# A fused gated cross-attention and expert layer: the first attention's keys made by a weight product, another order on every engine, zeros from another queue

## The chip, the core and the metric

The kernel runs on one core of one Trainium2 chip. The metric is the device time of one execution in microseconds (us), the median of several. A core has four engines that compute: TensorE (PE, matrix products; its weight loads are shown as PEld), VectorE (DVE), ScalarE (ACT) and GpSimd (POOL). A fifth, SyncE (SP), only issues transfers here. Each engine takes its own instructions in the order in which they are written, and waits on semaphores for the others.

## The reference

Eight sequences (B) of 256 tokens of width 256 pass four residual blocks. Each block normalises x first and is scaled by the tanh of a gain.

```python
x = x + tanh(g_xattn[0]) * L0_xattn(layernorm(x), ctx)   # one head, keys from ctx, 120 rows
x = x + tanh(g_ffn[0])   * L0_ffn(layernorm(x))          # 8 experts and 4 identities, best 2
x = x + tanh(g_xattn[1]) * L1_xattn(layernorm(x), ctx)   # 16 heads
x = x + tanh(g_ffn[1])   * L1_ffn(layernorm(x))          # rounded to 8 bits
# L0_xattn:
q = query @ Wq + bq;  k = key @ Wk + bk;  v = value @ Wv + bv
out = softmax(q @ k.T) @ v
```

The change is about the first line and what runs beside it. The scores are (xn Wq + bq)(ctx Wk + bk)^T. A term that is the same for all keys of a query drops out in the softmax.

## The kernel before, in words

Tokens lie on 128 partitions, two tiles (U) for a batch. Everything runs out of one program with a written order for each engine; a number t counts the iterations of a software pipeline, and each engine handles, in iteration t, steps of different batches.

**First attention.** For each batch b, TensorE makes keys `kt0` = Wk^T ctx (`keys0`, line 1549), which ScalarE copies out with the bias (`copy_kt0`, 622). Then TensorE multiplies them with Wq (`keys_by_query`, 1560) and with bq (1563), and VectorE copies the two results (`copy_kq`, 1006, `copy_bqk`, 1010). TensorE makes the values (1570), transposes the normalised x (1575, copied out by ScalarE in 629), and forms the scores (the bias row 1589, the product 1595). VectorE takes the maximum (1021), ScalarE the exponentials (635), TensorE transposes them (1604), ScalarE copies (642), TensorE multiplies with the values (1612), VectorE adds the result to x (1027, 1030).

**Norms.** VectorE makes mean and variance (986 to 994; `stats0` of x, `stats1` of x after the attention), GpSimd takes the root (496, 498; `root0`, `root1`), ScalarE applies it (648 for `norm0`, 657 for `norm1`). The second result is stored to HBM by SP, transposed (1575 again, copied by VectorE in 1041) and multiplied with the gate (1629); VectorE adds the gate's bias (1051) and has the logits.

**Choice of experts.** From the logits VectorE finds the two best experts of each token (`highest`, `mark_highest`, `keep_first`, `leave`; 1071 to 1083), for the first twelve tiles already inside the loop, for the last four and for the second choice after it. It forms `pairs` (1135), counts them with TensorE's help and turns them into slots (1175) and block numbers (1182). GpSimd then gathers the tokens of each of 39 blocks, TensorE runs the experts, and the second attention and the last layer follow.

**Beside it.** The expert weights (8 MB) come in eight loads of 1 MB from SP's queue. They are used as a sum of two parts, so they are split in 32 pieces of 512 columns: ScalarE writes the high part (`high`, 667), after the load, and GpSimd the low part (`low`, 512), after the high part; VectorE takes four of the low ones (1047). Which iteration takes how many pieces is written by hand (`HIGH_FROM`, `LOW_FROM`, `LOW_LATE`). The rows to which the experts' results are added start as zeros: ScalarE's queue writes them (`clear_y`), four transfers of 1 MB, in iteration 7. TensorE waits for all low parts behind the slot products, then issues a few products as a warm-up (1706), and reads the block numbers.

In iteration t the order before was as in the functions below. On ScalarE the first pieces stand in iteration 2, behind the normalisation of batches 0 and 1.

Of the kernel before, what the change touches and what calls it, by code (L numbers as in the profile page):

```python
# [90 lines left out]
def build(nc, x, ctxT, wq0T, wk0, wv0, bq0, bk0, bv0, gateT, gbias, wmoe, wq1, wk1, wv1, wo1,  # L91
          bq1, bk1, bv1, bo1, wfT, bf, gains, c_ident, c_tri, c_count, c_token, c_head, out):
    ctx = ExitStack()
    with ctx:
# [87 lines left out]
        kt0 = sb("kt0", [P, 2, C, LK], F32, att)  # L182
# [111 lines left out]
        def sems(names):  # L294
# [11 lines left out]
        (kt_done, kt_ok, kq_done, kq_ok, bqk_ok, v0_done, v0_ok) = sems(  # L306
            "kt_done kt_ok kq_done kq_ok bqk_ok v0_done v0_ok")
# [7 lines left out]
        split_h, split_l, split_d = sems("split_h split_l split_d")  # L315
# [80 lines left out]
        IN_CTX, IN_CON, IN_CST = 16 * 3, 16 * 4, 16 * 6  # L396
# [9 lines left out]


        HIGH_FROM, LOW_FROM = (8, 2, 2, 2), (4, 4, 9, 3)
        EARLY, FAR = TILES - 2 * U, 64 * P
        AHEAD, ZERO_LOADS = 6, 1 + 2 * TILES * D // ZEROS  # L410
        VECTOR_LOW, VECTOR_FROM = (7, 10, 13, 16), 5
        LOW_LATE = {B: 3, B + 1: 4, B + 2: 3, B + 3: 2, B + 4: CHUNKS}

        @block.sync
        def _(sp):
# [58 lines left out]
        def _(pool):  # L474
            pool.dma_start(ident[:], c_ident).then_inc(cst_in, 16)
# [38 lines left out]
            pieces = iter(j for j in range(CHUNKS) if j not in VECTOR_LOW)  # L514

            def low_next(t, k):

                if t >= LOW_FROM[k]:
                    for j in itertools.islice(pieces, 1):
                        low(j)  # L520

            for t in range(B):
                low_next(t, 0)
                low_next(t, 1)
                root0(t)
                low_next(t, 2)
                low_next(t, 3)
                if 0 <= t - 5:
                    root1(t - 5)
            for t in range(B, B + 5):  # L530
                root1(t - 5)
                for j in itertools.islice(pieces, LOW_LATE[t]):
                    low(j)
# [73 lines left out]
        def _(act):  # L607
# [10 lines left out]
            def copy_kt0(b):  # L618
                act.wait_ge(kt_done, b + 1)
                wait(act, kq_done, b - 1)  # L620
                for m in range(C):
                    ins = nc.scalar.activation(kt0[:, b % 2, m, :], bank[5][:, m * LK:(m + 1) * LK], ACT.Identity,
                                               bias=bk0_sb[:, m:m + 1])
                ins.then_inc(kt_ok, 1)
# [46 lines left out]
            def high_next(t, k):  # L671

                if t >= HIGH_FROM[k]:
                    for j in itertools.islice(pieces, 1):
                        high(j)

            def clear_y():

                act.wait_ge(zero_ok, 1)
                act.dma_start(xn_d[0:1, :], wh[0:1, E_FFN * WE - D:].bitcast(F32)).then_inc(zeroed, 16)  # L680
                y_p = y_d[1:1 + 2 * TILES * P, :].rearrange("(p r) n -> p (r n)", p=P)
                for c in range(0, 2 * TILES * D, ZEROS):
                    act.dma_start(y_p[:, c:c + ZEROS], wh[:, E_FFN * WE - ZEROS:].bitcast(F32)).then_inc(zeroed, 16)

            for t in range(B + 9):
                if t == B - 1:
                    clear_y()
                if t < B:
                    copy_kt0(t)
                high_next(t, 0)  # L690
                high_next(t, 1)
# [7 lines left out]
                if 0 <= t - 3 < B:  # L699
                    copy_probT(t - 3)  # L700
                high_next(t, 3)
                if 0 <= t - 1 < B:
                    copy_xT(t - 1)
# [276 lines left out]
        def _(dve):  # L980
# [22 lines left out]
            def copy_kq(b):  # L1003

                dve.wait_ge(kq_done, b + 1)
                dve.tensor_copy(kq[:, cols(b, C * LK)], bank[1][:, 0:C * LK]).then_inc(kq_ok, 1)

            def copy_bqk(b):
                dve.wait_ge(kq_done, b + 1)
                dve.tensor_copy(bqk[0:1, cols(b, LK)], bank[1][0:1, C * LK:(C + 1) * LK]).then_inc(bqk_ok, 1)  # L1010

            def copy_v0(b):

                dve.wait_ge(v0_done, b + 1)
                dve.scalar_tensor_tensor(v0[:, b, 0:D], bank[4][0:LK, 0:D], gain[0:LK, 0:1], bv0g[0:LK, :], ALU.mult,
# [26 lines left out]

            def low(j):

                dve.wait_ge(split_h, j + 1)
                c = cols(j, CHUNK)
                dve.tensor_tensor(wl[:, c], wl[:, c].bitcast(F32), wh[:, c], ALU.subtract).then_inc(split_d, 1)
# [37 lines left out]
            for t in range(B + 9):  # L1085
                if t < B:
                    stats0(t)
                if 0 <= t - 3 < B:
                    copy_bqk(t - 3)
# [1037 lines left out]
```

## Time and profile before

| | us |
|---|---|
| median of 3 runs | 392.32 (391.3 to 392.92) |
| the profiled execution: its own time | 393.37 |
| its span, first to last instruction | 391.6 |
| last logits added | 77.8 |
| block numbers ready | 91.5 |

Busy shares of the span: PE 89%, PEld 69%, DVE 68%, ACT 59%, POOL 41%. Shares of the chain that ended last: PE 71%, DVE 9%, ACT 8%, DMA 5%, waiting for issue 4%. The weight loads move 413 to 439 GB/s while they run.

A row of the chain names what the end of the program hung on at that moment. A row in order of time gives start, length, engine, line, tile written and tiles read, and in brackets how long the engine had stood idle before and what released it. "x4" means four instructions merged in one row. An fp32 product is two passes of TensorE, and two instructions in the trace. Granted clock is a share of 2.4 GHz.

### The profile page before, as it was taken

To read this page: it belongs to the slowest core of one execution; us is meant where nothing else is said; L and a number is where in the kernel's file an instruction comes from. 1 tells how busy PE (TensorE), PEld (TensorE's weight loads), DVE (VectorE), ACT (ScalarE), POOL (GpSimd) and SP (SyncE) were. 2 spreads that over 40 slices of the span, in tenths; PEclk is the share of its full clock that TensorE was granted. 3 is DMA by queue.
4 is the path that set the end of the run, shared out by engine and by line. 5 is a ranking of instruction groups with operands and counts; after the bars stand their busy time and mean duration, and the time that the engine had idled before them with its cause. 6 is when DMAs were issued, how large, how long until landed. Compare 5 with 4: busy or idle time off the path is not lost.

```text
span 391.6 us, 9083 instructions
## 1 busy us (share of the span) xinstructions
PE 347.3 (89%) x2955; PEld 268.6 (69%) x2956; DVE 266.0 (68%) x677; ACT 230.8 (59%) x462; POOL 159.2 (41%) x215
## 2 busy tenths in 40 slices
PE   1979999966899999999999998879999999989174
PEld 1768878644688888888888884556666666756142
DVE  1637887894645665555454456878889988685896
ACT  2387799530455555555555542466778678747685
POOL 6386589703255555555556524421132033001000
PEclk9969999975899999999999999999999999999776
DMA  7998381311132343423322304310011000000014
GB/s 191 329 419 332 145 365 57 110 28 40 40 95 94 108 133 103 123 68 80 80 73 67 87 30 145 112 56 22 35 56 55 2 2 2 3 2 2 0 42 175
DMA packets 15387, 38.26 MB, mean 98 GB/s; under 512 B 3574, under 2 KB 4748, under 8 KB 13820
## 3 DMA queue, kind: packets, MB, share of 16 engines
q1 hardware_dynamic: 9978, 22.55, 16.2%
q0 software_dynamic: 3936, 10.45, 9.2%
q10 hardware_dynamic: 1442, 4.85, 3.2%
q8 instruction: 19, 0.31, 0.4%
q14 instruction: 12, 0.10, 0.1%
HBM read 24.34 MB, written 13.50 MB: 97 GB/s over the span
## 4 chain that ended last, share of the span: by engine, by line
PE 71%; DVE 9%; ACT 8%; DMA 5%; issue 4%; ACTq 1%; SPq 1%; POOL 0%; DVEq 0%
PE two L1738 14%; PE two L1872 5%; PE two L1726 5%; PE two L1727 5%; PE two L1728 5%; PE two L1757 4%; PE two L1937 4%; PE two L1902 4%; PE two L1858 3%; PE two L1838 3%; DMA wl<-in_wmoe 3%; PE two L1748 2%; PE two L1929 2%; PE two L1595 1%; ACT wh L667 1%
## 5 line engine op out<-in xcount | busy, mean ns | idle before, releaser
L539 POOL DMA_INDIRECT xg<-xn_d,slot_i x39 | 37.8, 968 | 65.3 <-PE two L1748 51.1
L1222 DVE SCALAR_TENSOR_TENSOR gate<-th,two 128x512 f32<-128x512 f32 x39 | 26.8, 687 | 42.8 <-ACT th L738 42.8
L1726 PE MATMUL two<-wh,gh 128*128 x156 | 47.3, 303 | 0.2
L545 POOL DMA_INDIRECT y_d<-y_sb,goal_i x39 | 38.5, 988 | 20.5 <-ACT y_sb L748 10.5
L738 ACT ACTIVATE th<-two 128x512 f32<-128x512 f32 x39 | 23.3, 597 | 35.5 <-PE two L1738 35.5
L1727 PE MATMUL two<-wl,gh 128*128 x156 | 44.0, 282 | 0.0
L1728 PE MATMUL two<-wh,gl 128*128 x156 | 43.9, 282 | 0.0
L1757 PE MATMUL two<-ident,gate 128*128 128x128 f32 x156 | 41.9, 272 | 0.0
L559 POOL TENSOR_TENSOR rstd<-var,half 128x2 f32<-128x2 f32 x14 | 9.8, 701 | 76.7 <-DVE var L1289 76.7
L1322 DVE TENSOR_REDUCE nm<-two 128x8 f32<-128x960 f32 x32 | 36.1, 1151 | 4.5 <-PE two L1858 4.1
L512 POOL TENSOR_TENSOR wl<-wl,wh 128x512 fp32r<-128x512 f32 x28 | 35.2, 1275 | 9.8 <-ACT wh L667 9.8
L1738 PE MATMUL two<-wl,xh 128*128 x78 | 38.0, 487 | 0.0
L1738 PE MATMUL two<-wh,xl 128*128 x78 | 37.9, 485 | 0.0
L1738 PE MATMUL two<-wh,xh 128*128 x78 | 35.0, 449 | 2.1 <-DVE xl L1216 2.1
L836 ACT ACTIVATE pT<-two 120x1024 f32<-120x1024 f32 x32 | 31.1, 1036 | 7.0 <-PE two L1872 7.0
L1216 DVE TENSOR_TENSOR xl<-two,xh 128x256 fp32r<-128x256 f32 x39 | 16.6, 425 | 23.2 <-ACT xh L733 23.1
L1726 PEld LDWEIGHTS two<-wh,gh 128*128 128x128 f32 x156 | 29.5, 189 | 3.3 <-issue 0.7
L1727 PEld LDWEIGHTS two<-wl,gh 128*128 128x128 f32 x156 | 29.7, 190 | 0.0
L1728 PEld LDWEIGHTS two<-wh,gl 128*128 128x128 f32 x156 | 29.6, 190 | 0.0
L733 ACT ACTIVATE xh<-two 128x256 fp32r<-128x256 f32 x39 | 15.0, 384 | 23.2 <-PE two L1748 23.1
L1226 DVE TENSOR_TENSOR gl<-two,gh 128x512 fp32r<-128x512 f32 x39 | 26.6, 683 | 0.8 <-ACT gh L743 0.8
L748 ACT ACTIVATE y_sb<-two 128x256 f32<-128x256 f32 x39 | 15.0, 384 | 19.7 <-PE two L1728 19.0
(267 smaller groups left out, 892.0 us busy)
## 6 DMA issues: line engine op xcount, KB each, us to landing
wl<-in_wmoe SPq DMA_DIRECT2D x8, 1024.0 KB, 14.5
y_d<-wh ACTq DMA_DIRECT2D x4, 1024.0 KB
yg<-y_d SPq DMA_DIRECT2D x7, 512.0 KB, 3.6
xn_d<-xq SPq DMA_DIRECT2D x8, 256.0 KB, 2.0
xz<-xn_d SPq DMA_DIRECT2D x8, 256.0 KB, 2.6
out_x<-of SPq DMA_DIRECT2D x8, 256.0 KB, 2.0
x_sb<-in_x SPq DMA_DIRECT2D x1, 1024.0 KB, 7.9
x_sb<-in_x SPq DMA_DIRECT2D x1, 768.0 KB, 4.5
```

Of the source, the lines that this page charges most:

```text
L512: pool.tensor_tensor(wl[:, c], wl[:, c].bitcast(F32), wh[:, c], ALU.subtract).then_inc(split_l, 1)
L539: pool.indirect_dma_start(xg[:, n % 2, :], None, xn_d, bass.IndirectOffsetOnAxis(ap=slot_i[:, n:n + 1], axis=0)).then_inc(gathered[n % 2], 16)
L545: pool.indirect_dma_start(y_d, bass.IndirectOffsetOnAxis(ap=goal_i[:, n:n + 1], axis=0), y_sb[:, n % 2, :], None).then_inc(y_stored[n % 2] ...
L836: nc.scalar.activation(pT[:, r, p, :], ring(ring_of_keys(b, r) + p)[0:LK, :], ACT.Exp).then_inc(e_ok, 1)
L1222: dve.scalar_tensor_tensor(gate[:, k, :], th[:], 1.0, bank[2 + k][:], ALU.add, ALU.mult).then_inc(gate_ok, 1)
L1226: dve.tensor_tensor(gl[:, k, :], bank[4 + k][:], gh[:, k, :], ALU.subtract).then_inc(gl_ok, 1)
L1322: dve.tensor_reduce(nm[:, u, 2 * HG * p:2 * HG * (p + 1)].rearrange("p (j h) -> p j h", j=2), src.rearrange("p j (h k) -> p j h k", k=LK), ...
L1726: pe.matmul(dst, gh[:, k, a], wh[:, bass.ds(w, D)], start=c == 0, stop=False)
L1727: pe.matmul(dst, gh[:, k, a], wl[:, bass.ds(w, D)], start=False, stop=False)
L1728: ins = pe.matmul(dst, gl[:, k, a], wh[:, bass.ds(w, D)], start=False, stop=c == FC - 1)
L1738: ins = pe.matmul(bank[2 + k][:], (xl if part == 2 else xh)[:, k, c * P:(c + 1) * P], (wl if part == 1 else wh)[:, bass.ds(e + c * FF, FF) ...
L1757: ins = pe.transpose(bank[4 + k][:, c * P:(c + 1) * P], gate[:, k, c * P:(c + 1) * P], ident[:])
```

## The change

It does five things.

- **Keys.** At the start TensorE transposes Wk, forms Wk Wq^T (`qk`, with Wk bq as its last column) and the small bias terms, and then makes the keys of all batches in two products of 480 columns for each half of the width, and the bias row in two more (`fold_keys`, `keys0`). VectorE copies half of it out and ScalarE the other half (`copy_fold`, `copy_kq0`, `copy_kq1`). The work for each batch in `keys0`, `keys_by_query`, `copy_kt0`, `copy_kq` and `copy_bqk` goes away. The identity gets a semaphore of its own.
- **Order.** The loops of TensorE, ScalarE and VectorE are written anew. Steps follow one another at fewer iterations of distance (B + 7 in place of B + 9), and VectorE makes the first statistics four batches ahead.
- **High pieces** of ScalarE: the counts for each iteration are the list `HIGHS`; the first piece now stands in iteration 0 ahead of `norm0(0)`.
- **Low pieces** all go to GpSimd. It takes the roots of batches 0 to 4 first, two pieces ahead of each of the roots 5 to 7, the pieces of the list `LOWS` between the roots of the second norm, and all that are left behind the last root.
- **Zeros.** SP's queue writes them, between the fifth and the sixth weight load.

In the diff, runs of removed lines are left out; they stand in the functions above.

```diff
+        HIGHS = (1, 1, 2, 2, 2, 2, 1, 1, 3, 3, 3, 3, 3, 3, 2)
+        LOWS = (2, 2, 1, 1, 1, 2, 2)
...
+                if m == LOADS // 2:
+                    sp.wait_ge(zero_ok, 1)
+                    sp.dma_start(xn_d[0:1, :], wh[0:1, E_FFN * WE - D:].bitcast(F32)).then_inc(zeroed, 16)
+                    y_p = y_d[1:1 + 2 * TILES * P, :].rearrange("(p r) n -> p (r n)", p=P)
+                    for c in range(0, 2 * TILES * D, ZEROS):
+                        sp.dma_start(y_p[:, c:c + ZEROS], wh[:, E_FFN * WE - ZEROS:].bitcast(F32)).then_inc(zeroed, 16)
...
+            pieces = iter(range(CHUNKS))
+            def low_next(n):
+                for j in itertools.islice(pieces, n):
                     low(j)
+            for b in range(5):
+                root0(b)
+            for b in range(5, B):
+                low_next(2)
+                root0(b)
+            for b in range(B):
+                if b:
+                    low_next(LOWS[b - 1])
+                root1(b)
+            for j in pieces:
+                low(j)
...
+            def copy_kq1():
+                act.wait_ge(fold_ok, 3)
+                for h in range(2):
+                    act.wait_ge(fold_done, 6 + h)
+                    nc.scalar.activation(keys_of_half(1, h), bank[4 + h][:, 0:HB].rearrange("p (b k) -> p b k", k=LK),
+                                         ACT.Identity, bias=kq_bias[:, 1:2]).then_inc(kq1_ok, 1)
...
+            def high_next(n):
+                for j in itertools.islice(pieces, n):
+                    high(j)
+            for t in range(B + 7):
                 if 0 <= t - 3 < B:
-                    exp0_of(t - 3)
+                    copy_probT(t - 3)
+                high_next(HIGHS[t])
                 if 0 <= t - 6 < B:
                     norm1(t - 6)
-                high_next(t, 2)
+                if 0 <= t - 1 < B:
+                    copy_xT(t - 1)
+                if t == 1:
+                    copy_kq1()
+                if 0 <= t - 2 < B:
+                    exp0_of(t - 2)
                 if t < B:
                     norm0(t)
...
+            def copy_fold():
+                dve.wait_ge(fold_done, 1)
+                dve.tensor_copy(wkT[:].rearrange("p c n -> p (c n)"), bank[5][:, 0:C * P]).then_inc(fold_ok, 1)
+                dve.wait_ge(fold_done, 2)
+                dve.tensor_copy(qk[:], bank[0][:, 0:D + 1]).then_inc(fold_ok, 1)
+                dve.wait_ge(fold_done, 3)
+                dve.tensor_copy(kq_bias[:, 0:C], bank[7][:, 0:C])
+                dve.tensor_copy(kq_bias[0:1, C:C + 1], bank[7][0:1, C:C + 1]).then_inc(fold_ok, 1)
+            def copy_kq0():
+                dve.wait_ge(fold_ok, 3)
+                for h in range(2):
+                    dve.wait_ge(fold_done, 4 + h)
+                    dve.tensor_scalar(keys_of_half(0, h), bank[2 + h][:, 0:HB].rearrange("p (b k) -> p b k", k=LK),
+                                      kq_bias[:, 0:1], None, ALU.add).then_inc(kq_ok, 1)
+                for h in range(2):
+                    dve.wait_ge(fold_done, 8 + h)
+                    dve.tensor_scalar(bqk[:, h * HB:(h + 1) * HB], bank[6 * h][0:1, 0:HB], kq_bias[0:1, C:C + 1], None,
+                                      ALU.add).then_inc(kq_ok, 1)
 
...
+            for t in range(-4, B + 7):
+                if t == 0:
+                    copy_kq0()
                     dve.wait_ge(wv_in, 32)
                     dve.wait_ge(gain_ok, 1)
                     own.mark(dve.tensor_tensor(bv0g[:], bv0_sb[:], gain[:, 0:1].to_broadcast([P, D]), ALU.mult))
@@ -1095,32 +1094,32 @@
                     dve.wait_ge(cst_in, IN_CST)
                     dve.tensor_tensor(before[:], over(count[:, 0:E_FFN], E_FFN), wide(count[:, 0:E_FFN], E_FFN),
                                       ALU.is_lt)
...
+                if 0 <= t < B:
+                    copy_v0(t)
+                if t == 7:
                     dve.wait_ge(gate_in, 32)
...
+                if 0 <= t - 7 < B:
+                    logits_of(t - 7)
+                if t == B + 4:
                     dve.wait_ge(logit_kept, EARLY // U)
                     highest(0, lg, 0, EARLY)
                     mark_highest(0, lg, 0, EARLY)
-                if t == B + 7:
+                if t == B + 5:
                     keep_first(0, 0, EARLY)
                     leave(0, EARLY)
                     highest(1, left, 0, EARLY)
                 if 0 <= t - 5 < B:
-                    stats1(t - 5)
+                    copy_xT1(t - 5)
                 if 0 <= t - 2 < B:
...
+                    stats1(t - 2)
+                if 0 <= t < B:
+                    max0_of(t)
+                if t + 4 < B:
+                    stats0(t + 4)
+                if t == -4:
+                    copy_fold()
+                if 0 <= t - 1 < B:
+                    add_x1(t - 1)
...
+            def fold_keys():
+                pe.wait_ge(ident_in, 16)
+                for c in range(C):
+                    ins = pe.transpose(bank[5][:, c * P:(c + 1) * P], wk0_sb[:, c * P:(c + 1) * P], ident[:])
+                ins.then_inc(fold_done, 1)
+                pe.wait_ge(wq_in, 32)
+                pe.wait_ge(fold_ok, 1)
+                for c in range(C):
+                    pe.matmul(bank[0][:, 0:D], wkT[:, c, :], wq0_sb[:, c, :], start=(c == 0), stop=(c == C - 1))
+                for c in range(C):
+                    ins = pe.matmul(bank[0][:, D:D + 1], wkT[:, c, :], bq0_sb[:, c:c + 1], start=(c == 0), stop=(c == C - 1))
+                ins.then_inc(fold_done, 1)
                 for m in range(C):
                     for c in range(C):
-                        pe.matmul(bank[1][:, m * LK:(m + 1) * LK], wq0_sb[:, c, m * P:(m + 1) * P], kt0[:, b % 2, c, :],
-                                  start=(c == 0), stop=(c == C - 1))
+                        pe.matmul(bank[7][:, m:m + 1], wq0_sb[:, c, m * P:(m + 1) * P], bk0_sb[:, c:c + 1], start=(c == 0),
+                                  stop=(c == C - 1))
                 for c in range(C):
...
+                    ins = pe.matmul(bank[7][0:1, C:C + 1], bq0_sb[:, c:c + 1], bk0_sb[:, c:c + 1], start=(c == 0),
+                                    stop=(c == C - 1))
+                ins.then_inc(fold_done, 1)
+            def keys0():
+                pe.wait_ge(fold_ok, 3)
+                for m in range(C):
+                    for h in range(2):
+                        pe.matmul(bank[2 + 2 * m + h][:, 0:HB], qk[:, m * P:(m + 1) * P], ctxT_sb[:, h * HB:(h + 1) * HB],
+                                  start=True, stop=True).then_inc(fold_done, 1)
+                for h in range(2):
+                    pe.matmul(bank[6 * h][0:1, 0:HB], qk[:, D:D + 1], ctxT_sb[:, h * HB:(h + 1) * HB], start=True,
+                              stop=True).then_inc(fold_done, 1)
...
+            fold_keys()
+            keys0()
+            for t in range(B + 7):
+                if t == B + 2:
+                    pe.wait_ge(con_in, IN_CON)
+                if 0 <= t - (B + 2) < 3:
+                    products1(t - (B + 2), t - (B + 1))
+                if 0 <= t - 6 < B:
+                    transpose_x1(t - 6)
+                if 0 <= t - 2 < B:
+                    transpose_prob(t - 2)
+                if 0 <= t - 1 < B:
+                    scores0(t - 1)
+                if t == 0:
+                    pe.wait_ge(set_up, 1)
+                if t < B:
+                    transpose_x0(t)
+                if 0 <= t - 2 < B:
+                    attend(t - 2)
+                if t == 0:
+                    pe.wait_ge(wv_in, 32)
+                if t < B:
+                    values0(t)
+                if t == 7:
                     pe.wait_ge(gate_in, 32)
...
                 if 0 <= t - 7 < B:
-                    transpose_x1(t - 7)
+                    gate_of(t - 7)
```

## Rows read from the trace of the kernel before

**Rows 1.** Chain of waits, 0 to 115 us: start us, us, what (x instructions)

```profile
9.50 9.94 DMA wl<-in_wmoe
...
31.36 0.44 PE two L1575 x4
31.80 0.89 PE two L1560 x8
32.69 0.50 PE two L1563 x4
33.19 0.36 PE two L1604 x2
...
33.99 0.44 PE two L1549 x4
34.43 0.60 PE two L1589 x2
35.02 1.08 PE two L1595 x8
...
36.98 0.44 PE two L1575 x4
...
54.75 0.81 PE two L1629 x8
...
70.04 0.81 PE two L1637 x2
```

**Rows 2.** Windows of 10 us: busy time of each engine, granted clock, DMA

```profile
20.00:30.00 10.00, 7.95 (x39) 6.32 (x38) 2.67 (x11) 8.12 (x20) 8.92 (x9) 0.66 1.01 422
```

**Rows 3.** Order in time on ScalarE, 58 to 64 us: start, us, instruction

```profile
58.62 0.59 ACT L629 ACTIVATE xT<-two 128x512 f32<-128x512 f32 x1
...
60.37 0.61 ACT L635 ACTIVATE prob<-two,negmax 128x120 f32<-128x120 f32 x2
60.88 1.08 ACT L657 ACTIVATE xq<-x_sb,less,rstd 128x256 f32<-128x256 f32 x2
...
62.38 0.37 ACT L642 ACTIVATE probT<-two 120x256 f32<-120x256 f32 x1
62.64 1.66 ACT L667 ACTIVATE wh<-wl 128x512 fp32r<-128x512 f32 x3
```

**Rows 4.** Order in time on VectorE, 52 to 58 us

```profile
53.92 0.69 DVE L1041 COPY xT<-two 128x512 f32<-128x512 f32 x1 [0.50 <-PE two L1575]
...
54.99 0.87 DVE L1030 SCALAR_TENSOR_TENSOR x_sb<-two,rsum,x_sb 128x256 f32<-128x256 f32 x2
...
55.90 0.75 DVE L986 BATCH_NORM_STATS2 stat<-x_sb 128x6 f32<-128x256 f32 x2
...
57.05 0.14 DVE L994 TENSOR_REDUCE var<-mean 128x2 f32<-128x4 f32 x1
```

**Rows 5.** Order in time on GpSimd, 70 to 75 us

```profile
71.70 0.69 POOL L496 TENSOR_TENSOR rstd<-var,half 128x2 f32<-128x2 f32 x1
72.47 0.20 POOL L498 TENSOR_TENSOR less<-less,rstd 128x2 f32<-128x2 f32 x1
72.62 1.27 POOL L512 TENSOR_TENSOR wl<-wl,wh 128x512 fp32r<-128x512 f32 x1
...
73.85 1.33 POOL L512 TENSOR_TENSOR wl<-wl,wh 128x512 fp32r<-128x512 f32 x1
```

**Rows 6.** Order in time on VectorE, 73 to 82 us

```profile
73.33 0.30 DVE L1071 TENSOR_REDUCE top<-logit 128x12 f32<-128x144 f32 x1
73.67 0.40 DVE L1074 TENSOR_TENSOR eq<-logit,top 128x144 f32<-128x144 f32 x1
...
74.09 1.26 DVE L1075 SCALAR_TENSOR_TENSOR cand<-eq,count 128x144 f32<-128x144 f32 x1
...
80.03 0.36 DVE L1075 SCALAR_TENSOR_TENSOR cand<-eq,count 128x192 f32<-128x192 f32 x1
...
81.20 0.29 DVE L1135 TENSOR_TENSOR pairs<-hot 128x128 bf16<-128x128 f32 x1
```

More of the change, by code:

```diff
@@ L512, in low @@
                 pool.tensor_tensor(wl[:, c], wl[:, c].bitcast(F32), wh[:, c], ALU.subtract).then_inc(split_l, 1)
[L514 to L532, printed above, removed]
-                    low(j)
+            pieces = iter(range(CHUNKS))
+            def low_next(n):
+                for j in itertools.islice(pieces, n):
+                    low(j)
+            for b in range(5):
[9 more added lines that the diff above has]
+                low(j)
             pool.wait_ge(slots_kept, 1)
@@ L616, in _ @@
             act.wait_ge(ctx_in, IN_CTX)
[L618 to L624, printed above, removed]
+            def copy_kq1():
[4 more added lines that the diff above has]
+                                         ACT.Identity, bias=kq_bias[:, 1:2]).then_inc(kq1_ok, 1)
             def copy_xT(b):
@@ L1083, in leave @@
                 then(dve.scalar_tensor_tensor(left[:, i:n], hot[:, 0, i:n], -3.0e38, lg[:, i:n], ALU.mult, ALU.add))
[L1085 to L1089, printed above, removed]
-                if t == 3:
+            for t in range(-4, B + 7):
+                if t == 0:
+                    copy_kq0()
                     dve.wait_ge(wv_in, 32)
@@ L1544, in _ @@
             pe.wait_ge(ctx_in, IN_CTX)
-            def keys0(b):
-                wait(pe, kt_ok, b)
-                for m in range(C):
-                    ins = pe.matmul(bank[5][:, m * LK:(m + 1) * LK], wk0_sb[:, m * P:(m + 1) * P], ctxT_sb[:, cols(b, LK)],
-                                    start=True, stop=True)
-                ins.then_inc(kt_done, 1)
-            def keys_by_query(b):
-                pe.wait_ge(kt_ok, b + 1)
-                wait(pe, kq_ok, b)
-                wait(pe, bqk_ok, b)
+            def fold_keys():
[10 more added lines that the diff above has]
+                ins.then_inc(fold_done, 1)
@@ L1558, in keys_by_query @@
                 for m in range(C):
                     for c in range(C):
-                        pe.matmul(bank[1][:, m * LK:(m + 1) * LK], wq0_sb[:, c, m * P:(m + 1) * P], kt0[:, b % 2, c, :],
-                                  start=(c == 0), stop=(c == C - 1))
+                        pe.matmul(bank[7][:, m:m + 1], wq0_sb[:, c, m * P:(m + 1) * P], bk0_sb[:, c:c + 1], start=(c == 0),
+                                  stop=(c == C - 1))
                 for c in range(C):
-                    ins = pe.matmul(bank[1][0:1, C * LK:(C + 1) * LK], bq0_sb[:, c:c + 1], kt0[:, b % 2, c, :],
-                                    start=(c == 0), stop=(c == C - 1))
@@ L1567, in values0 @@
             def values0(b):
                 wait(pe, v0_ok, b)
-                wait(pe, xT1_copied, b - 5)
-                pe.matmul(bank[4][0:LK, 0:D], ctxT_sb[:, cols(b, LK)], wv0_sb[:], start=True, stop=True).then_inc(v0_done, 1)
+                pe.matmul(bank[1][0:LK, 0:D], ctxT_sb[:, cols(b, LK)], wv0_sb[:], start=True, stop=True).then_inc(v0_done, 1)
             def transposes(dst, src):
```

112 lines of the change are left out of this document (15 added, 97 removed).

## The prediction, made before the changed kernel was run

> **What bounds the kernel now.** I read the page first (the table above), then the chain of waits, then the order in time on each engine between 20 and 92 us, because the diff touches nothing behind that. The first attention with its gate ends at 77.8 us, a chain of VectorE instructions turns the logits into a list of slots and blocks until 91.5, and then TensorE runs the experts almost without a gap. So the change is worth what it moves the moment at which block numbers are ready and the split weights are whole. Inside the attention the reader should see the chain stay on TensorE from 31 to 42 us: one batch takes 5.62 us (transposes start at 31.36 and again at 36.98) and the engine does not stop between them [rows 1]. Before that the chain hangs on a load: the first of the eight weight loads lands at 19.44 [rows 1], and behind this wait TensorE's clock drops to the 1.2 GHz level for a while: granted 0.66 between 20 and 30 us [rows 2]. After that stretch it is at 2.4 GHz.
>
> **Part 1, keys for all batches ahead.** Per batch TensorE loses the key product by query (0.89), its bias row (0.50) and the raw key product (0.44) [rows 1]: 1.83 of 5.62, so 3.79 remains, 14.6 for eight batches. What comes instead is done once: two transposes, the 128x257 product, twelve one-column matmul passes, and six products of 480 columns. One like these takes 0.81 (the row at 70.04, one product in two passes [rows 1]), so 4.9 at 2.4 GHz, at most twice that at 1.2; the small ones I put at 3 to 5, from the 0.50 of the four bias passes, doubled. Starting at about 6 (identity and first weights are in by then) they end between 14 and 21; I take 18.6. It costs nothing if it ends before 21.1, for this reason: in iteration 0 ScalarE now has a first piece of the weight split ahead of the normalisation of batch 0, and that piece waits for the load that lands at 19.44. Before, two batches were normalised by then. So batch 0 is transposed from 21.1, behind an idle TensorE, at the low clock. With the key copies of ScalarE (two of 480 columns, some 0.65 each) ahead of the scores I get scores(0) complete at 27.1; between the bounds 25.8 (high clock) and 28.
>
> **Part 2, the loop from there.** The order is now tighter. Between the end of one batch's scores and the next stand: transpose of the next x, ScalarE's copy of it (0.59), exponentials (0.61), transpose of the probabilities (about 0.36), bias row and scores (0.60 + 1.08) [rows 1, 3], with semaphores about 4.0. ScalarE itself has, per iteration, 0.37 + 0.59 + 0.61, a normalisation of 1.08 and from batch 6 on a second one, and the split pieces at 0.55 each in a row [rows 3]; that is 3.6 to 4.2. VectorE has in iterations 2 and 3 two sets of statistics (55.90 to 57.19, so 1.29 each), the residual (0.87 and a reciprocal) and some 0.9 of small work [rows 4]: 4.5. TensorE has 3.79, and 5.04 once the second transpose (0.44) and the gate (0.8) join. Taking the longest each time, and the waits between engines in the written order, the seven intervals are 4.5, 3.8, 4.2, 4.6, 4.8, 4.2 and 5.1: scores(7) complete at 58.3. Before it was at 63.9, so the attention gains 5.6 there. Then a part is given back: three split pieces stand in each of ScalarE's iterations 8 to 13. From the last exponentials (60.3) it has 0.9 (wait and copy) + 1.7 + 1.1, then three times 1.7 + 1.0: the last normalised x1 is out at 72.0. Transpose (0.65), copy (0.69 [rows 4]), gate (1.0) and add bring the last logits to 74.6, against 77.8: 3.2 earlier. ScalarE alone bounds it below: it has some 45.5 of work from 19.4 to that last normalisation, so no earlier than 65 plus 2.6. VectorE loses its four split pieces, but they lie beside TensorE's work. The zeros go from ScalarE's queue to SP's, between the fifth and sixth load. They are 4 MB, about 10 us at the 413 GB/s of the table, so the last loads land near 50 and the pieces in them are wanted from 61 on; this costs nothing, and ScalarE need not issue them. SP's stores of x1 start at about 46, behind these loads, and are wanted two batches later.
>
> **Part 3, GpSimd's order, where I see the price.** Before, it had done 25 of its 28 pieces when the last root was taken at 71.70. Now it has all 32. The root of batch 4 waits for statistics that VectorE makes behind the first maximum, near 28.9, so nothing is split before that. Up to the last root, 6 + 11 = 17 pieces are placed: all 15 others stand behind root 7. That root needs the last x1's statistics; in VectorE's order they stand behind the copy of batch 4's transpose, so the root starts at about 67.3 and ends at 68.2 to 68.4 (0.69 + 0.20 with gaps [rows 5]). 15 pieces of 1.27 to 1.33 [rows 5] run till 87.9 at least, all through the chain of VectorE that chooses the experts, which before had GpSimd silent from 76.5.
> Does that matter? The trace shows it at one place. GpSimd's pieces run from 72.62 to 73.89 and from 73.85 to 75.18 [rows 5]. VectorE's equality begins at 73.67 and ends at 74.07, 0.2 behind the end of the first; the next operation begins at 74.09 and ends at 75.35, again 0.2 behind the end of the second: 1.26 us for 144 columns, where the same line does 192 columns in 0.36 with GpSimd silent [rows 6]. The reduction ahead of them, and copies out of PSUM at other times, are not stretched. So an instruction of that kind is let in once per piece. GpSimd loses only 0.03 to 0.06 by it.
> The Trainium skill (SBUF — State Buffer, section "Who interferes with whom") says that a VectorE instruction with two SBUF inputs and a GpSimd instruction that reads SBUF exclude each other for a whole instruction, while a reduction is outside of this. The trace agrees in the two operations above (1.26 against 0.36). By the rows alone only the equality and the multiply-add are proven to be stopped, which would be 6 instructions of the stage; by the rule the products and differences too, 12 in all. With six the total below would be about +2 instead of +7.
> I take all that read two SBUF tiles, since the equality is the same instruction type as the others. Early part: equality and multiply-add (iteration 12) end at about 72.5 and 73.8; the copy of the last transpose stands behind them, 74.5; equality and difference of iteration 13 at 76.4 and 77.7; the last logits are added at 78.2 instead of 74.6. Of the 3.2 nothing is left (+0.4). Late part, from there: eight such instructions in a row of dependence (equality, multiply-add, mark, leave, difference, equality, multiply-add, mark), one per 1.30, with the reductions inside these gaps: 79.0, 80.3, 81.6, 82.9, 84.2, 85.5, 86.8, 88.1. By then GpSimd is done, and the pairs are formed at 88.2 instead of 81.20 [rows 6]. All behind it is as before.
> **Sum:** +7.0 on the profiled execution (393.4 us by its own time, span 391.6), which was 1.05 above the median. On the median of 392.3 that is 399.3, so 399. The end of GpSimd's pieces (87.9) isn't waited for then: slots would be ready at 96.9.
>
> **Rivals.**
> *A: the two engines hardly meet; faster.* For it: two stretched instructions are few, and the attention's gain may be larger. Then the blocks are ready 3.2 earlier, at 88.3. TensorE waits for all pieces ahead of its warm-up, at 87.9, and that just fits. Time: 392.3 - 3.2 = 389. It decides where fewer than about four of the twelve are stopped (they cost 10.2 together in my sum, 0.85 each). Against it: both meetings of that kind in this stretch end with GpSimd's piece.
> *B: the attention reaches ScalarE's bound,* last logits up to 7 earlier than in my walk, with the blocking in full: 399.3 - 7 = 392, no change. It would need ScalarE never to wait, where the first scores alone hold it for 3.
> *C: the clock.* TensorE now stands still between 18.6 and 21.1 and works in pieces until 29. If it stays at the low level for two iterations more, each has 7.6 instead of some 4.2: +6.8, so 406. For it: the 0.66 in the stretch behind the wait for the first load [rows 1, 2]. Against: with full work it was at the high level again by 29.
> *D: half of the instructions are stopped,* or GpSimd is a few pieces ahead: +1 to +3, so about 394.5.
>
> **Chances.** Forecast 0.58 (own range 395.5 to 403), A 0.17, B 0.07, C 0.10, D 0.08. Within 0.5% is 390.3 to 394.3, about what a measurement here can tell from no change: faster is A, same is B and part of D. The range goes from 389.5 to 405: it takes in most of A, and C with one and a half cold iterations.
>
> **What would show it.** Right: the last GpSimd piece ends near 88; the row of that multiply-add shows over 1 us at several places and the chain from the last logits to the pairs takes near 10 us instead of 3.4; the last normalised x1 at 72; first transpose of x at 21. Wrong: a chain of 3.4 again with GpSimd still busy (the mechanism falls), GpSimd done before 80 (the order in time falls), or granted clock under 0.9 after 30 us (C).

## The result, and the profile after

| | before | after |
|---|---|---|
| median, us | 392.44 (4 runs, 391.3 to 392.9) | 397.73 (4 runs, 396.5 to 401.7) |
| ratio, with its 95% interval | | 1.0158 [1.012, 1.0196] |
| span of the profiled execution | 391.6 | 399.9 |
| last logits added, start | 77.65 | 75.48 |
| pairs formed, start | 81.20 | 85.27 |
| last low piece of GpSimd ends | 76.5 | 86.4 |
| block numbers ready, start of the last instruction | 91.31 | 96.66 |

The change is slower by 5.3 us (397.73 against 392.44). 399 was forecast. Ratios, here and below, are formed from fast executions alone and are not the quotient of the two medians. The profiled execution after is the longest of its four, so its span shows 8.3 us more; the stage that the change touches accounts for 5.35 of them (block numbers), and this is what the medians differ by. The other 3 lie behind it (last part of this section).

First VectorE in order of time, in the changed kernel (start, us, engine, line, what). It answers to [rows 6].

```profile
70.74 0.41 DVE L1076 TENSOR_TENSOR eq<-logit,top 128x144 f32<-128x144 f32 x1
71.18 1.27 DVE L1077 SCALAR_TENSOR_TENSOR cand<-eq,count 128x144 f32<-128x144 f32 x1
...
73.51 0.31 DVE L1082 TENSOR_TENSOR hot<-cand,pick 128x144 f32<-128x144 f32 x1
73.85 1.26 DVE L1085 SCALAR_TENSOR_TENSOR left<-hot,logit 128x144 f32<-128x144 f32 x1
75.15 0.30 DVE L1073 TENSOR_REDUCE top<-left 128x12 f32<-128x144 f32 x1
75.48 0.18 DVE L1053 TENSOR_TENSOR logit<-two,gbias_sb 128x24 f32<-128x24 f32 x1
...
75.94 0.36 DVE L1076 TENSOR_TENSOR eq<-logit,top 128x48 f32<-128x48 f32 x1
76.34 1.19 DVE L1077 SCALAR_TENSOR_TENSOR cand<-eq,count 128x48 f32<-128x48 f32 x1
77.56 0.20 DVE L1081 TENSOR_REDUCE pick<-cand 128x4 f32<-128x48 f32 x1
77.80 0.96 DVE L1082 TENSOR_TENSOR hot<-cand,pick 128x48 f32<-128x48 f32 x1
78.79 1.19 DVE L1085 SCALAR_TENSOR_TENSOR left<-hot,logit 128x48 f32<-128x48 f32 x1
...
80.25 0.92 DVE L1131 TENSOR_TENSOR dif<-top 128x16 f32<-128x16 f32 x1
81.09 1.48 DVE L1076 TENSOR_TENSOR eq<-left,top 128x192 f32<-128x192 f32 x1
82.60 1.30 DVE L1077 SCALAR_TENSOR_TENSOR cand<-eq,count 128x192 f32<-128x192 f32 x1
...
84.33 0.91 DVE L1082 TENSOR_TENSOR hot<-cand,pick 128x192 f32<-128x192 f32 x1
85.27 1.23 DVE L1134 TENSOR_TENSOR pairs<-hot 128x128 bf16<-128x128 f32 x1
...
96.66 0.18 DVE L1181 SCALAR_TENSOR_TENSOR blk_i<-blk,blks 128x20 int32<-128x20 f32 x1
```

Then GpSimd in the same kernel, as [rows 5]: the last root, and the first and last of the pieces behind it.

```profile
66.33 0.69 POOL L508 TENSOR_TENSOR rstd<-var,half 128x2 f32<-128x2 f32 x1 [0.53 <-DVE var L989]
...
67.25 8.99 POOL L524 TENSOR_TENSOR wl<-wl,wh 128x512 fp32r<-128x512 f32 x7
...
82.32 4.04 POOL L524 TENSOR_TENSOR wl<-wl,wh 128x512 fp32r<-128x512 f32 x3
```

The reader should see that between 71 and 86.5 us the equality (1076), multiply-add (1077), mark (1082), leave (1085), difference (1131) and pairs (1134) take 0.9 to 1.5 us, where with GpSimd silent 0.2 to 0.4 is their length. GpSimd runs its 15 pieces through just this time, from 67.25 to 86.36. Of the twelve instructions that the prediction counted, nine are stopped in full. The equality at 70.74 (0.41) meets the end of a piece, the mark at 73.51 (0.31) is not held, and the equality at 75.94 takes 0.36, where 0.21 was its length before. The pairs at 85.27 are stopped too (1.23 for 0.29) and make a tenth. The reductions between them (1073, 1081) keep their 0.2 to 0.3. From the start of the last logits to that of the pairs it takes 9.8 us; before it took 3.55.

The chain of waits of the changed kernel, start of the loop and the scores of batches 0, 1, 2 and 7 (start, us, what), to be read against [rows 1]:

```profile
9.38 10.22 DMA wl<-in_wmoe
...
19.68 0.63 ACT wh L676
20.31 0.99 ACT xq L657 x2
...
21.44 0.64 PE two L1585 x4
...
22.60 1.22 ACT kq L632 x2
...
24.59 1.16 PE two L1605 x8
...
29.57 1.99 PE two L1605 x8
...
36.17 1.10 PE two L1605 x8
...
57.12 1.08 PE two L1605 x8
```

The first weight piece on ScalarE waits for the load, and the norm of batch 0, its transpose and the key copies follow it. Scores(7) are complete at 58.2. And the granted clock (columns: stretch, length, busy us and count of PE, PEld, DVE, ACT, POOL; granted clock, DMA share, GB/s), against [rows 2]:

```profile
20.00:24.00 4.00, 1.79 (x9) 0.76 (x7) 2.37 (x5) 3.71 (x8) 0.00 (x0) 1.00 1.01 420
24.00:28.00 4.00, 3.66 (x17) 2.62 (x18) 2.02 (x8) 3.18 (x8) 0.53 (x1) 0.68 1.00 416
28.00:32.00 4.00, 4.00 (x16) 3.07 (x16) 0.40 (x2) 2.02 (x5) 2.81 (x4) 0.50 1.01 422
32.00:36.00 4.00, 4.00 (x12) 2.76 (x11) 2.94 (x13) 2.63 (x7) 2.64 (x4) 0.54 1.01 428
```

TensorE works 1.8 us of the 4 from 20 to 24, and then runs at the 1.2 GHz level until about 35.7, without a pause from 28 on. Before, the low stretch was over at 29. The same happens once more: in the window from 100 to 110 us, where the experts begin, the clock is 0.63 after the change, and 0.97 was granted from 100 to 110 before. These are different moments of the work (the experts begin 5.3 later), but between block numbers and the end the span is 303.2 after and 300.3 before. In ten of the twelve kernels below that distance is 300.1 to 301.6 (in the other two 301.9 and 302.0), so these 3 us are not taken as the change's. No run shows what decides them.

### The profile page after: what moved, and what is told of

Its sections match the earlier page's. It is cut to its first block, busy times and chain, and to the rows that moved or that the text cites. A ratio compares the mean times of both kernels' runs of the same rounds, so it can differ in the third digit from the quotient of the medians.

```text
span 399.9 us, 8859 instructions
## 1 busy us (share of the span) xinstructions
PE 353.4 (88%) x2861; PEld 266.9 (67%) x2862; DVE 270.5 (68%) x665; ACT 227.8 (57%) x448; POOL 164.0 (41%) x219
## 4 chain that ended last, share of the span: by engine, by line
PE 70%; DVE 12%; ACT 7%; DMA 5%; issue 3%; POOL 1%; SPq 1%; ACTq 0%; DVEq 0%
PE two L1736 14%; PE two L1870 5%; PE two L1724 5%; PE two L1725 5%; PE two L1726 5%; PE two L1755 4%; PE two L1900 4%; PE two L1935 4%; PE two L1856 4%; PE two L1836 3%; DMA wl<-in_wmoe 3%; PE two L1746 2%; PE two L1605 2%; PE two L1927 2%; PE two L1585 1%
## 5 line engine op out<-in xcount | busy, mean ns | idle before, releaser
L524 POOL TENSOR_TENSOR wl<-wl,wh 128x512 fp32r<-128x512 f32 x32 | 40.5, 1292 | 0.0
```

Source lines behind the costliest of these rows:

```text
L524: pool.tensor_tensor(wl[:, c], wl[:, c].bitcast(F32), wh[:, c], ALU.subtract).then_inc(split_l, 1)
```

## Experiments

Each expectation stands as it was given before the run. Times are medians; ratios are to the kernel before, which was measured again beside each group of kernels, with medians of 392.45, 392.76 and 391.96. So a difference of 1 or 2 us between two of the kernels below is not shown by their times; where the text rests on one, it gives the moments in the traces too. "Block numbers" is the start of the last instruction that makes them, as in the table.

**The 15 pieces left out.**

```diff
             for j in pieces:
-                low(j)
+                pool.wait_ge(split_h, j + 1)
+            pool.memset(spare_sb[:, 0:1], 0.0).then_inc(split_l, 15)
```

> The changed kernel without the 15 low pieces behind GpSimd's last root: they are left out (those columns of the low part stay unsplit), all else as it is. Theory (VectorE's choice of experts is stopped by GpSimd's pieces): the twelve instructions take 0.2 to 0.4 us each again instead of about 1.2, the pairs are formed near 77, block numbers near 87.5 instead of 96.7, so about 388.5 us. Rival 1 (the attention itself gained nothing, the loss is the clock or the new order): blocks no earlier than 95, 396 to 398. Rival 2 (half the loss is elsewhere): 393.

391.2 us (10 runs, 385.7 to 394.2), 0.9976 [0.9944, 1.0007]. VectorE in this kernel, same instructions as above:

```profile
70.06 0.21 DVE L1078 TENSOR_TENSOR eq<-logit,top 128x48 f32<-128x48 f32 x1
70.30 0.21 DVE L1079 SCALAR_TENSOR_TENSOR cand<-eq,count 128x48 f32<-128x48 f32 x1
...
71.59 0.35 DVE L1078 TENSOR_TENSOR eq<-left,top 128x192 f32<-128x192 f32 x1
71.98 0.36 DVE L1079 SCALAR_TENSOR_TENSOR cand<-eq,count 128x192 f32<-128x192 f32 x1
...
73.15 0.29 DVE L1136 TENSOR_TENSOR pairs<-hot 128x128 bf16<-128x128 f32 x1
```

All are back at 0.21 to 0.36, and the pairs come 3.55 us behind the last logits. From the end of ScalarE's last norm to the block numbers it takes 16.8 us here (66.55 to 83.30) and 25.5 in the changed kernel (71.17 to 96.66). These 8.7 us are 1.3 ahead of the last logits, 6.2 in the late chain, 0.9 in the pairs' own row and 0.3 behind it. The medians differ by less, 6.5 us, not by the 9.2 expected. The runs spread over 8 us, and their mean granted clock goes from 0.922 to 0.946. The profiled one was the fastest (385.7), with a granted clock of 1.00 from 20 to 60 us and the last logits at 69.6, so that trace is not that of the median run. Why the medians show less stays open.

**The same pieces as writes.**

```diff
             for j in pieces:
-                low(j)
+                pool.wait_ge(split_h, j + 1)
+                own.mark(pool.memset(wl[:, cols(j, CHUNK)].bitcast(F32), 0.0))
+                own.settle()
+                pool.memset(wl[:, cols(j, CHUNK)].bitcast(F32), 0.0).then_inc(split_l, 1)
```

> The same 15 pieces replaced by GpSimd instructions that only write (two fills of 512 columns each, some 1.2 us together, values not the reference's). GpSimd stays busy till about 85 as in the changed kernel. Theory with the rule of the Trainium skill (only a GpSimd instruction that reads SBUF excludes one of VectorE with two SBUF inputs): VectorE runs free, blocks near 87.5 to 88, about 389 us. Rival (any work of GpSimd on SBUF stops VectorE, or what costs is only that TensorE waits for GpSimd's end): 395 to 398.

390.7 us (6 runs), 0.9925 [0.9885, 0.9965]. VectorE, and two of the 30 fills of GpSimd in the same time:

```profile
77.38 0.21 DVE L1080 SCALAR_TENSOR_TENSOR cand<-eq,count 128x48 f32<-128x48 f32 x1
...
79.06 0.36 DVE L1080 SCALAR_TENSOR_TENSOR cand<-eq,count 128x192 f32<-128x192 f32 x1
...
80.24 0.29 DVE L1137 TENSOR_TENSOR pairs<-hot 128x128 bf16<-128x128 f32 x1
```

```profile
76.31 0.52 POOL L544 MEMSET wl<- 128x512 f32 x1
...
77.94 0.52 POOL L546 MEMSET wl<- 128x512 f32 x1
```

GpSimd is busy until 84.8, and in the chain VectorE is not held once: it takes 3.57 us. So what stops these instructions is GpSimd reading, as the theory had it, and neither GpSimd's work as such nor TensorE's wait for its end costs the 7 us. (Behind the chain one instruction with a single SBUF input, line 1156, took 0.27 for 0.18 and ended at 84.80, as the last fill did at 84.76. One row proves little.) (The profiled execution was granted 0.69 and 0.63 from 20 to 40 us and took 395.2; the other five took 388.2 to 394.6.)

**20 pieces behind the last root.**

```diff
-        LOWS = (2, 2, 1, 1, 1, 2, 2)
+        LOWS = (1, 1, 1, 1, 1, 1, 0)
```

> The changed kernel with LOWS = (1, 1, 1, 1, 1, 1, 0): 20 pieces behind the last root instead of 15. Theory: GpSimd ends near 93 instead of 86.4, and three or four further instructions with two SBUF inputs are stopped for about 0.9 us each: 400.5 to 401.5. Rival (TensorE's wait for the pieces is the loss): GpSimd's end at 93 is still ahead of the slots at 95.2, so no change, 397.7.

401.3 us (4 runs), 1.0189 [1.0145, 1.0233]. By the medians that is +3.6 on the changed kernel, but the intervals of the two ratios overlap (1.0158 there), so the times alone do not show it. The traces do: block numbers start at 100.21 instead of 96.66. Of these 3.5 us, 1.1 lie ahead of the last logits (76.56), in an execution with a longer low stretch of the clock (0.66 from 20 to 40 us, 0.74 there). The chain to the pairs takes 9.8 as before, and 2.5 lie behind the pairs. GpSimd ends at 93.8, still ahead of the slots (98.8), so TensorE's wait is not the cause. The rows of VectorE behind the pairs:

```profile
87.95 0.82 DVE L1139 TENSOR_SCALAR prod<-valid 128x32 f32<-128x32 f32 x1
88.66 0.67 DVE L1141 TENSOR_REDUCE red<-wf_sb 128x1 f32<-128x512 f32 x1
...
89.44 0.57 DVE L1147 SCALAR_TENSOR_TENSOR ahead<-rows_up,before 128x64 f32<-128x64 f32 x1
...
90.62 0.81 DVE L1150 TENSOR_TENSOR prod<-hot,place 128x256 f32<-128x256 f32 x1
...
91.96 0.64 DVE L1153 TENSOR_SCALAR up<-pos 128x32 f32<-128x32 f32 x1
92.64 1.19 DVE L1154 TENSOR_SCALAR col<-up 128x32 f16<-128x32 f32 x1
```

The next instructions are now stopped as well: 1147 takes 0.57 and 1150 takes 0.81, where the changed kernel has 0.22 and 0.42. One thing was not in the theory: 1139, 1153 and 1154 have a single SBUF input, and take 0.82, 0.64 and 1.19 for 0.20, 0.18 and 0.18. These three make 2.1 of the 2.8 us by which the five are longer.

**That part of the change alone, in the kernel before.**

```diff
-        LOW_LATE = {B: 3, B + 1: 4, B + 2: 3, B + 3: 2, B + 4: CHUNKS}
+        LOW_LATE = {B: 0, B + 1: 0, B + 2: 0, B + 3: 0, B + 4: CHUNKS}
```

> The kernel before with only LOW_LATE changed, so that 15 of its 28 pieces on GpSimd stand behind the last root, as in the changed kernel. Attention, keys and zeros as before. Theory: last logits near 78, GpSimd busy till about 91.5, the pairs formed near 88.5 to 90 instead of 81.2, blocks near 100 instead of 91.5: 400 to 402 us. Rival (GpSimd's late pieces are harmless, the loss comes from the new attention): 392, as before.

400.9 us (4 runs), 1.0183 [1.0141, 1.0224]. The last logits start at 77.44, almost as before, GpSimd's pieces end at 89.6, and VectorE shows the same lengths as in the changed kernel:

```profile
83.04 1.48 DVE L1074 TENSOR_TENSOR eq<-left,top 128x192 f32<-128x192 f32 x1
84.55 1.30 DVE L1075 SCALAR_TENSOR_TENSOR cand<-eq,count 128x192 f32<-128x192 f32 x1
...
87.22 1.23 DVE L1135 TENSOR_TENSOR pairs<-hot 128x128 bf16<-128x128 f32 x1
```

Only the places of GpSimd's pieces were changed, and the kernel before loses 8.4 us in the median (7.2 by the ratio) and 7.6 in the block numbers (98.89 for 91.31). That is more than the whole change loses by the medians (5.3) and by the block numbers (5.35), so the rest of the change gives something back. How much is not well fixed: 3 us by the medians, 2.2 by the block numbers, while the intervals of the two ratios overlap. The kernel with writes in place of the reads, 0.9925 of the kernel before, says the same from the other side.

**Half pieces.**

```diff
             for j in pieces:
-                low(j)
+                pool.wait_ge(split_h, j + 1)
+                for n in range(2):
+                    c = cols(2 * j + n, CHUNK // 2)
+                    ins = pool.tensor_tensor(wl[:, c], wl[:, c].bitcast(F32), wh[:, c], ALU.subtract)
+                ins.then_inc(split_l, 1)
```

> The changed kernel with only the 15 low pieces behind the last root cut in halves of 256 columns (30 instructions). Theory (one VectorE instruction with two SBUF inputs per GpSimd instruction): the rows of such instructions show 0.5 to 0.7 instead of 0.9 to 1.5, the chain from the last logits to the pairs takes 6 to 7 us instead of 10.9, GpSimd ends near 88; block numbers near 92.5 instead of 96.7: 393 to 394. Rival (the port is shared over time, so the sum of GpSimd's work counts and not its cut): 397 to 398.

394.9 us (7 runs), 1.010 [1.006, 1.0141].

```profile
74.71 0.65 DVE L1081 SCALAR_TENSOR_TENSOR cand<-eq,count 128x48 f32<-128x48 f32 x1
...
76.08 0.65 DVE L1089 SCALAR_TENSOR_TENSOR left<-hot,logit 128x48 f32<-128x48 f32 x1
...
79.88 0.69 DVE L1138 TENSOR_TENSOR pairs<-hot 128x128 bf16<-128x128 f32 x1
```

The same work of GpSimd, cut finer, stops VectorE for half as long: 0.65 where it was 1.19, and 6.4 us for the chain. GpSimd needs 22.0 us instead of 19.1, so more work in all stops VectorE less. So the wait lasts until the end of the GpSimd instruction that is running, as [rows 5, 6] had shown at two places. The block numbers start at 92.71, 3.9 earlier than in the changed kernel; 2.0 of that lie ahead of the last logits, in an execution whose clock was less low (0.83 from 20 to 40 us, 0.74 there). Part of the chain's gain is given back: GpSimd goes on to 87.4, six instructions behind the pairs are held as well (1154, the 1150 of the changed kernel, takes 0.96 for 0.42), and from the pairs to the block numbers it takes 12.8 us instead of 11.4.

**The start of the loop and the clock.** Two edits of the changed kernel. First the norms ahead of the pieces:

```diff
-        HIGHS = (1, 1, 2, 2, 2, 2, 1, 1, 3, 3, 3, 3, 3, 3, 2)
+        HIGHS = (0, 0, 2, 2, 3, 3, 1, 1, 3, 3, 3, 3, 3, 3, 2)
```

> The changed kernel with HIGHS = (0, 0, 2, 2, 3, 3, 1, 1, 3, 3, 3, 3, 3, 3, 2): no piece of the split ahead of the norms of batches 0 and 1 and of ScalarE's key copies, so that they do not wait for the first load. Theory (the start of the loop hangs on that load): scores of batch 0 complete near 22.5 to 23 instead of 25.7, the attention 2 to 3 us earlier, more if TensorE's clock stays high; 395. Rival (ScalarE's later iterations with three pieces or the stop of VectorE set the end anyway): 397 to 398.

397.1 us (6 runs), 1.0113 [1.0076, 1.0149]: no gain that the times show, 1.5 us in the block numbers (95.15). The first maximum starts at 24.23 instead of 25.79, so the load was in the way by 1.6, less than the 3 expected. But TensorE still has its holes, the low clock comes from 24 us on and lasts to about 34, and the last logits start at 73.97, 1.5 earlier. The theory was right in kind and twice too large.

Second, filler products:

```diff
+            def idle(n):
+                for _ in range(n):
+                    pe.matmul(bank[3][:, 0:HB], wk0_sb[:, 0:P], ctxT_sb[:, 0:HB], start=True, stop=True,
+                              skip_group_check=True)
...
                 if t == 0:
                     pe.wait_ge(set_up, 1)
+                    pe.wait_ge(kq_ok, 2)
+                    idle(1)
...
                     values0(t)
+                if t < 2:
+                    idle(2 - t)
```

> The changed kernel with four filler products of 480 columns on TensorE in the holes of its iterations 0 and 1 (one ahead of the first transpose, two and one behind the values), results unused. Theory of the clock (TensorE runs at the 1.2 GHz level from 25.5 to about 35 us because it stood still between 20 and 24): the level stays at 2.4 GHz, the loop is some 4 us earlier, 393 to 395, with less spread between runs. Rival (the low level comes whatever the holes hold, or the fillers are in the way): 397 to 400.

395.9 us (6 runs, 395.7 to 397.6), 1.0089 [1.0059, 1.0119]. Windows of this kernel:

```profile
24.00:28.00 4.00, 4.00 (x22) 2.53 (x21) 1.93 (x8) 3.55 (x9) 0.33 (x1) 1.00 1.02 424
...
32.00:36.00 4.00, 4.00 (x24) 2.85 (x22) 3.83 (x18) 3.64 (x10) 3.26 (x5) 1.00 1.02 428
```

The clock stays at the 2.4 GHz level where it was 0.68 to 0.54, the last logits start at 72.01 (3.5 earlier), and the spread between runs is 2 us instead of 5. The median falls by only 1.8 (2.7 by the ratios), short of the 393 to 395 that the theory gave, the profiled span by 5.9 and the block numbers by 3.5. So taking the low stretch away gives the median some 2 to 3 us, what the fillers themselves take included, and 3.5 in the profiled execution, up to the block numbers.

**Zeros back on ScalarE's queue**, issued at its iteration 6 (the block of five transfers moved from the load loop, unchanged).

> The changed kernel with only the zeros back on ScalarE's queue, issued in its iteration 6. Theory of the prediction (who writes the zeros costs at most the issue): ScalarE loses about 2 us there while TensorE has work of the batch in hand; part of it is taken up by ScalarE's waits, so 397.7 to 399.5. Rival (zeros between the loads held the later loads and with them the pieces): 396 or less.

400.0 us (4 runs), 1.0211 [1.0159, 1.0263]: by the medians 2.3 slower than the changed kernel, with intervals that overlap. ScalarE there (idle before it, in brackets):

```profile
44.75 0.38 ACT L644 ACTIVATE probT<-two 120x256 f32<-120x256 f32 x1 [2.61 <-issue]
```

It stands idle for 2.6 us while it issues. But last logits and block numbers come only 0.6 later than in the changed kernel (76.05 and 97.23), in an execution whose clock was less low (0.83 from 20 to 40 us, 0.74 there). That the move of the zeros was worth about 2 us is likely and not shown; the prediction had booked no gain for it.

**Towards a faster version.** Eight pieces behind the last root, by taking more of them early:

```diff
-        HIGHS = (1, 1, 2, 2, 2, 2, 1, 1, 3, 3, 3, 3, 3, 3, 2)
-        LOWS = (2, 2, 1, 1, 1, 2, 2)
+        HIGHS = (1, 1, 4, 4, 4, 3, 1, 1, 2, 2, 2, 2, 2, 2, 1)
+        LOWS = (2, 2, 2, 2, 2, 2, 2)
...
-            for b in range(5):
-                root0(b)
-            for b in range(5, B):
-                low_next(2)
-                root0(b)
+            for b in range(B):
+                low_next((0, 0, 0, 0, 2, 3, 3, 2)[b])
+                root0(b)
```

> The changed kernel with the pieces moved forward on both engines: HIGHS = (1, 1, 4, 4, 4, 3, 1, 1, 2, 2, 2, 2, 2, 2, 1), two low pieces before root 4 of the first norm, then 3, 3, 2, and LOWS all 2, so 8 instead of 15 behind the last root. Nothing is left out. Theory: GpSimd ends near 77 to 78 instead of 86.4, some 6 of the 12 instructions are free again (about 0.8 each), and ScalarE's last iterations are shorter by 0.55 each: block numbers near 90 instead of 96.7, 390 to 392. Rival (the roots come late behind the pieces and hold ScalarE's second norm): no gain, 396 to 398.

393.0 us (10 runs), 0.9984 [0.9952, 1.0016]: 4.7 faster than the changed kernel, GpSimd done at 77.2, block numbers at 89.9. That is 1 us short of the range expected for the time (390 to 392), and right for the other two. In its trace the clock was less low, too (0.91 from 20 to 40 us), and 1.5 of the 6.8 us in the block numbers lie ahead of the last logits.

> Both of the two edits before together (HIGHS = (0, 0, 6, 4, 4, 3, 1, 1, 2, 2, 2, 2, 2, 2, 1)). Theory: the gains add up in part, 388 to 390, and the kernel is faster than the one before (392.4). Rival: six pieces in iteration 2 hold the copy of the second x and eat the earlier start, 392.

392.0 us (10 runs), 0.9979 [0.9952, 1.0006]. Block numbers at 87.6. The gains add up in part, but no difference from the kernel before is shown, where 388 to 390 was expected: the rival's time.

> The version with the norms first and eight pieces behind the last root, and the four filler products as well. Nothing of the result is left out. Theory: block numbers at 88.0 there; the fillers take away the 1.2 GHz stretch between 20 and 28 us and with it 1 to 2 us more: blocks near 86.5, 389 to 391, and faster than the kernel before (392.6) beyond its interval. Rival (ScalarE and VectorE set the pace from 28 us on, the clock gives nothing more): 392.

392.0 us (12 runs), 0.9996 [0.9974, 1.0017]: the rival. The clock is at its upper level from 20 to 40, yet the block numbers come at 89.0, later than without the fillers (87.6). The first transpose of x starts at 20.68 here and at 19.21 there. One filler product ahead of it takes 0.9 of that, the rest was there before the fillers. From 24 us on ScalarE is busy without a pause in both, as the rival had it.

> As that, and the eight low pieces behind the last root cut in halves of 256 columns. Theory (VectorE is let in once per GpSimd instruction): an instruction that is stopped waits for at most some 0.65 us instead of 1.27; five of them are stopped here, so about 2 us less than the version in whole pieces: 387.5 to 389.5. Rival (the start costs of 16 instructions on GpSimd, or it is let in less often than each time): no difference.

391.4 us (12 runs), 0.9993 [0.9973, 1.0013]. Block numbers at 87.9, 1.1 earlier than in whole pieces; less than the 2 expected, and in the time it is within the noise. The gain lies ahead of the last logits (71.40 for 73.10). The chain behind them is longer than in whole pieces, 6.15 us for 5.43, since GpSimd still works for 5.9 us of it and not for 3.2. No version with its whole work beat the kernel before beyond its interval.

## Why the prediction was right

- **The price is in GpSimd's order.** Right, and shown from four sides: without the reads (left out, or as writes) the loss of 5.3 is gone, with 20 pieces it is larger in the block numbers, with half pieces the chain is shorter, and in the kernel before the order of the pieces alone costs 7 to 8.
- **Which instructions are stopped.** All kinds that read two SBUF tiles, as taken, not only the two kinds whose rows had shown it. The rule about reads of the Trainium skill (SBUF — State Buffer, "Who interferes with whom") decided this, and the kernel with writes bears it out: 3.57 us for the chain beside a busy GpSimd. Nine of the twelve were stopped in full. The pairs, which also read two SBUF tiles, were stopped as well and had been left out, since GpSimd was thought to be done by then; instructions with one SBUF input were not thought of.
- **Where the size was off.** +7.0 was the sum, +5.35 the profile's. The term is the last logits: the walk had them added at 78.2, and it was 75.7 (start 75.48). The last norm left ScalarE at 71.2 instead of 72.0, and the stopped instructions ahead of the last logits cost 1.3 (the kernel without the pieces) where the walk had 3.6: the equality of iteration 12 met only the end of a piece (0.41), and the mark at 73.51 was let in at once. The late chain was sized well: 10.0 forecast, 9.8 measured. Taken apart and rounded, +5.35 is -2.2 (last logits), +6.2 (late chain), +0.9 (pairs) and +0.3 behind it. Here too errors partly cancelled: the last logits were 2.5 too late in the walk, and the pairs' own 0.9 was missing.
- **The attention.** Scores(7) at 58.3 forecast, 58.2 measured. That this fits to 0.1 is luck, for two errors cancelled: scores(0) were ready at 25.7, not 27.1, and the low clock lasted one iteration longer, so scores(2) came at 37.3, not 35.4. GpSimd's last root began at 66.3 (67.3).
- **Rivals.** A (the engines hardly meet) is excluded: nine meet in full. C (the clock) is there in part, and the sign that the prediction had named for it came: the granted clock from 30 to 40 us was 0.71, under 0.9. C's price of 6.8 did not: taking the low stretch away gave 2 to 3 us. B and D are excluded by the rows (last logits 2.2 earlier, not 7; more than half stopped).
- **Costs booked at nothing.** The zeros: moving them may have gained about 2 us, which the runs do not settle. It was part of the attention's gain and had no term of its own.
- **One lower bound.** The prediction has GpSimd's pieces run "till 87.9 at least". Its own figures, 15 pieces of 1.27 from 68.2, give 87.3 for the least; 86.4 was measured, as the root came earlier.

## What to carry to other kernels

Before work is handed to GpSimd "in the background", look at what VectorE does at that time: elementwise instructions with two SBUF inputs wait for the end of a GpSimd instruction that reads SBUF (1.19 us where 0.21 is the length alone), some with one SBUF input do too, and a chain of short ones then runs at GpSimd's pace. Put such background work beside VectorE's reductions and reads of PSUM, or cut it short. Even so, no order tried here brought the kernel below the one before. Freeing the busiest engine of a stage (here 14.6 us of TensorE, an estimate from [rows 1]) gives only what the next engine's written order allows, and holes in it can cost clock.

## What the runs showed of the hardware beside that

- GpSimd hardly pays for the meetings: 15 pieces took 19.1 us in the changed kernel, 1.27 each. VectorE alone waits, mostly one instruction per piece, and ends 0.15 to 0.2 behind the piece's end.
- A `tensor_scalar` with one SBUF input and fp32 from SBUF to SBUF was stopped as well (0.82 for 0.20 at 87.95, in the kernel with 20 pieces), and so was one that writes f16 (1.19 for 0.18 at 92.64), unlike the reductions between them (0.67, as always).
- TensorE was at the 1.2 GHz level until 18 us, 12 us after its first product, though it was busy for 4.00, 3.70 and 4.00 us of the three stretches of 4 us from 8 on. The key products of the changed kernel (eight passes of 480 columns, then four more):

```profile
12.43 6.55 PE L1572 MATMUL two<-ctxT_sb,qk 128*128 128x480 f32 x8 [0.30 <-DVE kq_bias L1006]
18.92 1.77 PE L1575 MATMUL two<-ctxT_sb,qk 128*1 128x480 f32 x4
```

The first eight take 0.82 each, the last four 0.44. The granted clock printed for this stretch is 1.00, so at the start of a trace the lengths are to be believed and not that column. The moment of the rise varies: the same eight passes, behind the same work, took 5.1 us in the kernel with both edits.
